# Experts' first layer: weights held, tokens streamed, so that its result comes out already turned

## What is computed

```python
logits = x @ gate_w.T                                   # 64 experts
topk_w, topk_idx = top_k(softmax(logits), 6)            # 6 experts a token, weights made to sum to 1
h = silu(einsum('th,eih->tei', x, experts_w1))          # first layer, 256 -> 176
y = einsum('tei,ehi->teh', h, experts_w2)               # second layer, 176 -> 256
out = sum over e of combine[t, e] * y[t, e]  +  shared expert
x = x + layernorm(out)
```

## Time and profile before

| | |
|---|---|
| time, three runs | 389.12 us median (386.97, 389.12, 392.39) |
| profiled execution, first to last instruction | 389.5 us (no other time is given for this execution) |
| PE, POOL, DVE, ACT busy | 298.0, 235.5, 197.3, 134.0 us |
| mean granted TensorE clock | 0.867 of 2.4 GHz |
| DMA moved | 55.99 MB, 144 GB/s over the span |

### The profile page before, as it was taken

How to read it: one execution, slowest core, us unless ns; L and a number is a source line. 1 busy time by engine, 2 the same in 40 slices (tenths; PEclk the granted TensorE clock), 3 DMA queues, 4 the chain that set the end, 5 groups by cost and what they waited for, 6 DMA issues and landing times.

```text
span 389.5 us, 5897 instructions
## 1 busy us (share of the span) xinstructions
PE 298.0 (76%) x1661; PEld 210.7 (54%) x1662; DVE 197.3 (51%) x552; ACT 134.0 (34%) x283; POOL 235.5 (60%) x248
## 2 busy tenths in 40 slices
PE   5759709479683989989999969969979799589400
PEld 4324607346442567667767757747756567356300
DVE  5338994786889457645343433323424143101176
ACT  1284540391530024333433424423333234223003
POOL 7008496050000074888888888888888888885452
PEclk9698957888879789999989989978999799968855
DMA  7994000100101024788887977878878788867763
GB/s 260 328 362 153 2 0 0 55 0 3 54 0 54 2 81 110 168 227 180 209 221 166 221 158 166 207 152 210 191 198 170 146 215 216 164 108 129 154 205 108
DMA packets 39236, 55.99 MB, mean 144 GB/s; under 512 B 4272, under 2 KB 28016, under 8 KB 39216
## 3 DMA queue, kind: packets, MB, share of 16 engines
q1 hardware_dynamic: 26544, 38.45, 31.6%
q0 software_dynamic: 12672, 17.31, 25.6%
HBM read 40.14 MB, written 15.60 MB: 143 GB/s over the span
## 4 chain that ended last, share of the span: by engine, by line
PE 34%; DMA 25%; DVE 17%; issue 12%; POOL 8%; ACT 3%; SPq 0%; POOLq 0%; DVEq 0%; ACTq 0%
DMA acc_rows<-yS,gat_idx 12%; DMA xg<-x_rows,gat_idx 11%; PE bank L687 5%; PE bank L837 5%; PE bank L846 4%; POOL acc_rows L487 4%; PE bank L747 4%; PE bank L845 3%; PE bank L703 3%; PE bank L856 3%; POOL xg L476 2%; PE bank L735 2%; DVE stats L922 2%; PE bank L695 2%; DMA work<-acc_rows 1%
## 5 line engine op out<-in xcount | busy, mean ns | idle before, releaser
L487 POOL DMA_INDIRECT acc_rows<-yS,gat_idx x66 | 106.7, 1617 | 27.4 <-issue 17.5
L476 POOL DMA_INDIRECT xg<-x_rows,gat_idx x66 | 69.2, 1049 | 47.2 <-DVE gat_idx L1134 31.1
L1203 DVE COPY hT<-bank 128x256 f32<-128x256 f32 x66 | 28.0, 425 | 131.9 <-PE bank L842 130.0
L655 ACT ACTIVATE yS<-bank,slot_sum 128x256 f32<-128x256 f32 x66 | 31.3, 474 | 74.1 <-PE bank L846 70.3
L837 PE MATMUL bank<-w_sb,xT 128*128 128x176 f32 x264 | 55.4, 337 | 0.0
L747 PEld LDWEIGHTS bank<-tslice,hit 128*128 128x128 bf16 x536 | 38.7, 167 | 29.6 <-issue 25.5
L846 PE MATMUL bank<-w2b_sb,hT 48*128 48x256 f32 x132 | 49.9, 461 | 0.0
L747 PE MATMUL bank<-tslice,hit 128*128 128x6 bf16 x536 | 43.5, 205 | 7.9 <-DVE tslice L1119 7.9
L1117 DVE TENSOR_TENSOR hit<-rank,slot_no 128x1024 bf16<-128x1024 bf16 x67 | 46.2, 689 | 1.9 <-PE bank L747 1.1
L856 PE MATMUL bank<-ident,xg 128*128 128x128 f32 x132 | 29.5, 307 | 21.3 <-DMA xg<-x_rows,gat_idx 21.2
L837 PEld LDWEIGHTS bank<-w_sb,xT 128*128 128x128 f32 x264 | 43.6, 207 | 0.9 <-issue 0.6
(11 more groups left out here) (162 smaller groups left out, 398.5 us busy)
## 6 DMA issues: line engine op xcount, KB each, us to landing
w_sb<-w SPq DMA_DIRECT2D x32, 608.0 KB, 4.5
acc_rows<-zeros SPq DMA_DIRECT2D x32, 128.0 KB, 4.3
w2b_sb<-w2b SPq DMA_DIRECT2D x32, 96.0 KB, 5.0
work<-acc_rows SPq DMA_DIRECT2D x8, 256.0 KB, 5.0
xg<-x_rows,gat_idx POOLq DMA_INDIRECT x66, 3.6
acc_rows<-yS,gat_idx POOLq DMA_INDIRECT x66, 4.7
x_sb<-x SPq DMA_DIRECT2D x4, 256.0 KB, 3.6
x_rows<-r SPq DMA_DIRECT2D x2, 512.0 KB, 2.8
```

The lines of the kernel that those rows point to most:

```text
L476: pool.indirect_dma_start(xg[:, c % 8, :], None, x_rows, bass.IndirectOffsetOnAxis(ap=gat_idx[:, (c // 4) % 4, c % 4:c % 4 + 1], axis=0)). ...
L487: pool.indirect_dma_start(acc_rows[acc_of(i, c)], bass.IndirectOffsetOnAxis(ap=gat_idx[:, (c // 4) % 4, c % 4:c % 4 + 1], axis=0), yS[:, c ...
L655: act.activation(yS[:, (c - 2) % 8, :], y_b[c % 2][:, 0:C], ACT.Copy, scale=slot_sum[:, ((c - 2) // 4) % 4, (c - 2) % 4, 1:2]).then_inc(y_ ...
L1203: dve.tensor_copy(hT[:, u].rearrange("p k t -> p (k t)"), hT_b[u][:, 0:2 * P]).then_inc(hT_done, 1)
```

## The change

The first layer's operands change places. The weights of the block are the stationary operand, in two pieces of 128 and 48 columns, and the tokens `xT` are the moving one, 128 columns. The result stands in PSUM already turned: the first 128 hidden units on the partitions of columns 0 to 127, the other 48 on partitions 0 to 47 of columns 128 to 255. ACT's silu reads all 256 columns and writes them straight into `hT`. `turn_hidden` and DVE's copy leave the pipeline, and the semaphores `hT_ps` and `hT_done` with them. The second layer of block s-1 is computed in step s, where it was that of block s-2. ACT's order and POOL's stay: yS of block s-2 is still written after silu of block s. (The old `hidden` and `turn_hidden` stay for the branch for further tokens, which does not run with these inputs.)

```diff
--- before.py
+++ after.py
@@ -127,7 +127,7 @@
         w2b_sb = sb("w2b_sb", [IR, 8, C])
         xg = sb("xg", [P, 8, C])
         xT = sb("xT", [P, 2, KC, P])
-        hS = sb("hS", [P, 2, I])
+        hS = sb("hS", [P, 1, I])
         hT = sb("hT", [P, 2, 2, P])
         yS = sb("yS", [P, 8, C])
         sq = work2[:].rearrange("p (b h) d -> p b (h d)", b=B).rearrange("p b (m t) -> p m b t", m=2)
@@ -206,8 +206,6 @@
         xT_done = sem("xT_done")
         h_ps = sem("h_ps")
         h_done = sem("h_done")
-        hT_ps = sem("hT_ps")
-        hT_done = sem("hT_done")
         y_ps = sem("y_ps")
         y_done = sem("y_done")
         scat = [sem(f"scat{j}") for j in range(ACCS)]
@@ -644,8 +642,9 @@
                 if exists(i, c):
                     act.wait_ge(h_ps, s + 1)
                     if later(i, c, 2):
-                        act.wait_ge(hT_ps, s - 1)
-                    act.activation(hS[:, c % 2, :], h_b[c % 2][:, 0:I], ACT.Silu).then_inc(h_done, 1)
+                        act.wait_ge(y_ps, s - 1)
+                    act.activation(hT[:, c % 2].rearrange("p k t -> p (k t)"), h_b[c % 2][:, 0:2 * P], ACT.Silu
+                                   ).then_inc(h_done, 1)
                 if exists(i, c - 2):
                     e = s - 2
                     act.wait_ge(y_ps, e + 1)
@@ -832,6 +831,14 @@
                 tables(0, e)
             pe.wait_ge(rank_read, 2)
 
+            def hidden_columns(dst, xTe, w):
+                for k in range(KC):
+                    pe.matmul(dst[:, 0:P], w[:, I * k:I * k + P], xTe[:, k, :], start=(k == 0), stop=(k == KC - 1))
+                for k in range(KC):
+                    mm = pe.matmul(dst[0:IR, P:2 * P], w[:, I * k + P:I * k + I], xTe[:, k, :],
+                                   start=(k == 0), stop=(k == KC - 1))
+                return mm
+
             def hidden(dst, xTe, w):
                 for k in range(KC):
                     mm = pe.matmul(dst, xTe[:, k, :], w[:, I * k:I * k + I], start=(k == 0), stop=(k == KC - 1))
@@ -866,18 +873,12 @@
                     pe.wait_ge(xT_done, s + 1)
                     if later(i, c, 2):
                         pe.wait_ge(h_done, s - 1)
-                    hidden(h_b[c % 2][:, 0:I], xT[:, c % 2], w12_sb[:, c % 8]).then_inc(h_ps, 1)
+                    hidden_columns(h_b[c % 2][:, 0:2 * P], xT[:, c % 2], w12_sb[:, c % 8]).then_inc(h_ps, 1)
                 if exists(i, c - 1):
                     u = c - 1
                     pe.wait_ge(h_done, s)
                     if later(i, c, 3):
-                        pe.wait_ge(hT_done, s - 2)
-                    turn_hidden(hT_b[u % 2][:, 0:2 * P], hS[:, u % 2]).then_inc(hT_ps, 1)
-                if exists(i, c - 2):
-                    u = c - 2
-                    pe.wait_ge(hT_done, s - 1)
-                    if later(i, c, 4):
-                        pe.wait_ge(y_done, s - 3)
+                        pe.wait_ge(y_done, s - 2)
                     output(y_b[u % 2][:, 0:C], hT[:, u % 2], w12_sb[:, u % 8], w2b_sb[:, u % 8, :]).then_inc(y_ps, 1)
                 if has_table(i, c + 9):
                     tables(i, c + 9)
@@ -1195,13 +1196,6 @@
                 s = TURN * i + c
                 if has_table(i, c + 9):
                     hits(i, c + 9)
-                if exists(i, c - 1):
-                    dve.wait_ge(hT_ps, s)
-                    if later(i, c, 3):
-                        dve.wait_ge(y_ps, s - 2)
-                    u = (c - 1) % 2
-                    dve.tensor_copy(hT[:, u].rearrange("p k t -> p (k t)"), hT_b[u][:, 0:2 * P]
-                                    ).then_inc(hT_done, 1)
                 if later(i, c, 0) and has_table(i, c + 8) and (c % 4 == 3 or not has_table(i, c + 9)):
                     sums(i, c + 8)
                 if isinstance(i, int):
```

## The result

The changed kernel takes **403.73 us** (median of 4 runs, 399.87 to 405.88); the kernel before, run beside it, 390.49 (386.97 to 392.39). The ratio is **1.0305 [1.0219, 1.039]**: slower. The forecast, no change at 389.5 us in a range of 382.5 to 395, was wrong. The profiled execution took 399.87 us, with a span of 398.1 us. It was the fastest of the four, so its profile shows less of the loss (8.6 us of span) than the medians do (13.2 us).

What follows compares the result with a forecast made beforehand. POOL's loop, 3.35 us a block, was taken as the limit, with PE's step of 2.83 us hidden beside it. Head +0.9 and tail -0.5 made +0.4 on the median 389.12: 389.5 us, no change, range 382.5 to 395.

Steps and rivals of the forecast that it cites:

- What bounds the kernel: Pipeline loop: POOL sets the pace at 3.35 us a block; PE needs 2.75 us a step and has 18.1 us of waits.
- The DVE copy: DVE in the loop: 66 copies, 28.0 us, go, and nothing gets faster but the start of `hit`.
- the second layer's place: Second layer one step up: no gain at the head, because ACT takes yS of block s-2 behind silu of block s.
- Rival A: PE's first layer: each weight load waits for the matmul ahead, 1.81 us, a step 3.74 us; 415 us in all; 3%.
- Rivals C and D: Loop: DVE's `hit` lengthens POOL's instructions less often (C, 382.5 us, 12%) or more often (D, 394.5 us, 8%).
- PE, first layer.: PE's step: eight matmuls replace four, 0.90 us for 0.60, so +0.30; with two turns gone, 2.83 us a step.
- The full clock came back each time while PE worked without them: PE's clock in the loop: it fell behind waits and recovered without them; argued against a lasting half clock.
- rival B: PE's clock: half clock for more than 25% of steps puts PE behind POOL for good; at 40%, 410 us; 6%.
- The head: Pipeline start: longer first layers and silu in the way, less the turns; first scatter at 151.2, not 150.31, +0.9 us.
- The tail: Pipeline end: yS of block 62 comes 0.3 us sooner; the tail gives back 0.5 of the 0.9, -0.5 us.

Runs made afterwards that it cites:

- wide_both: Changed kernel with the 48-column first-layer piece widened to 128 columns and `w2b_sb` to 128 rows; 389.02 us, ratio 0.9996.
- before_padded: Kernel before with one idle product of 256 columns in each PE step; 388.38 us, ratio 0.9985.
- after_again: Changed kernel, unedited, measured and profiled a second time; 394.39 us, ratio 1.0103.
- after_3: Changed kernel, unedited, measured a third time, in 6 runs; 406.23 us.
- late_output: Changed kernel with the second layer back at two blocks behind and four buffers of `hT`; 393.96 us, no ratio.
- early_ys: Changed kernel with ACT writing yS of block s-1 in step s, where it was s-2; 390.09 us, ratio 1.0024.
- wide_cols: Changed kernel with only the first layer's 48-column piece widened to 128, `w2b_sb` left at 48 rows; 389.76 us, ratio 1.0006.
- before_rows: Kernel before with `w2b_sb` widened to 128 rows, 80 of them zeros; 390.19 us, no ratio.
- warm_head: Changed kernel with five idle products of 256 columns in PE's step -1; 391.6 us, ratio 0.9968.
- after_padded: Changed kernel with one idle product of 128 columns in each PE step; 399.21 us, ratio 1.024.
- after: Changed kernel, unedited, in its first measurement and profile, against the kernel before; 403.73 us, ratio 1.0305.
- wide_96: Changed kernel with the first layer's second piece at 96 weight columns in place of 48; 391.48 us, ratio 1.0049.
- after_4: Changed kernel, unedited, measured a fourth time, in a single run; 403.72 us.

## Why the prediction was wrong, step by step

- **What bounds the kernel: right for the first profile, and only in part for the others.** POOL's loop runs at 6.70 us a turn before and 6.65 after, and no faster with a PE step of 2.47 us (wide_both, 6.73) than with 3.17 (before_padded, 6.57). But PE's cover was thinner than I had it. Behind a long stretch in the loop POOL waits for yS, 4.9 us in after_again and 3.5 in after_3, at 6.87 and 6.85 us a turn.
- **The DVE copy worth nothing, the second layer's place worth nothing: right.** DVE's 24 us went and nothing followed; late_output matches the unedited kernel. ACT's kept order was the reason, as early_ys shows.
- **Rival A, loads that do not hide: rightly put aside.** Eight loads and products take 0.90 us, 0.112 each (wide_both, wide_cols). The sentence on overlap that the prediction quotes from the Trainium skill ("TensorE: Matmul & The Clock Gate", Part 3, "The mechanism") would have given 1.81, and these runs disagree with it. The same section also says that a load into the background weight buffer is pulled ahead of matmuls in flight, which the prediction left out and with which these runs agree.
- **Rivals C and D, fewer or more collisions:** neither came; the turns are 6.65 us against 6.70.
- **The step that failed: "PE, first layer."** I priced "0.117 for the four with 128 weight columns and 0.109 for the four with 48", as if a narrower stationary operand could only be cheaper. Its size on the moving side was right: 0.90 us with 128 columns. But the 48-column group takes 0.57, not 0.44 or 0.45, and the 128-column product behind it 0.63, not 0.43: +0.30 us a step. The trace of before had shown the same kind of price: L846, with 48 rows, takes 0.63 where L845 takes 0.43, and the pair costs 0.35 in all, as before_rows and wide_both show (0.20 there, 0.15 in the tables behind it). I took those rows as they were and did not ask why two products of equal size differ. One row of before points the other way: L842, a turn with 48 stationary columns, has no extra price.
- **"The full clock came back each time while PE worked without them" (without waits): this carried the 6% for rival B, and it failed.** Rival B's mechanism is what happened, but in the first profile neither its place nor its condition. In the changed kernel the granted clock stayed at 0.5 (that is 1.2 GHz) to about 165 us, and from 142 us on the records show PE busy throughout. B asked for over 25% of the steps at half clock and PE as the loop's limit. The stretches of the profile come to 42 us, about 8 steps of 66 and no more than in the kernel before, and POOL stayed the loop's limit; they cost because 26 us of them are in one piece at the head, where POOL waits for PE.
- **The head: +0.9 us forecast; +5.4 to the first scatter and +10.9 to the first pace measured.** The terms were three first layers at 0.3 to 0.54. What they missed is that the head's clock was an outcome, not a given: I carried the 142 to 146 us stretch of before over unchanged. Without the long stretch it is still +3.5 (after_again), and +3.0 with the step as forecast (wide_cols), so the sum was too small there too.
- **The tail: -0.5 forecast, -0.2 measured.** Near enough, and of no weight.
- **What is shown and what is not.** Shown: the 48-column piece costs 0.30 us a step, and widening it (wide_cols, one edit) brings the time back; a step of that length without it does no such harm (before_padded). The narrow piece is needed for the loss but isn't enough for it: with it kept, the warm head takes away about half of the loss by the medians and all of it in the profiled run, and writing yS sooner (early_ys) brings the time back as well. Stretches of 26 to 36 us at half clock appear in five of the seven profiles of forms with the 48-column piece and no filling in each step (all four of the changed kernel, and late_output; not warm_head and early_ys), and in none of the eleven others, where the longest is 14 us (after_padded). Not shown is why the clock stays down in that form. after_padded was to test whether the make-up of the step decides it, and its 14 us at the head lie between the 8 and the 36 of the unfilled kernel, so it settles nothing.
- **The Trainium skill on this.** The Trainium skill ("TensorE: Matmul & The Clock Gate", "Why this matters for your kernels") ties the full clock to keeping the engine busy without a pause. Here the records show PE busy for 20.00 of 20.00 us at a granted clock of 0.51, so being busy by the records was not enough in this form (their ends are modelled, so short pauses may hide in them). That five idle products ahead of the head went with a clock of 1.00 there (warm_head, one profile) agrees with it.

## What to carry to other kernels

Price a matmul by its stationary shape too: if two products of equal stream differ in the trace, find out why before carrying the rows over. Padding the 48 columns and the 48 rows to 128, with zeros so placed that the result stays the same, took off 5.4 us beside the same kernel on the same chip. And treat the clock at the start of a pipeline as a result of the change, not as a constant: the steps there are paid at the clock that they get, and 0.3 us more a step at full clock went with 10.9 us at the loop's start in one profile and 3.5 in another. When one kernel gives 394 us once and 404 to 406 three times, take several profiles before you explain the first.

## What the runs showed of the hardware

At full clock, f32, the first layer's four matmuls with 48 stationary columns and 128 moving take 0.57 us and make the next pair 0.20 longer (after); with 96 or 128 columns they take 0.43 to 0.45 and cost the next one nothing (wide_96, wide_cols). A single turn with 48 stationary columns costs neither (L842 before: 0.11 us, and 0.43 for the pair behind it). A pair with 48 stationary rows takes 0.63 against 0.43 with 128 rows, and the bf16 products behind it 0.59 against 0.43 (after, wide_both). And the granted clock stayed at half for 24 us, and for about 35 in another profile, with no wait of PE in the records (after, after_4).
